# State space stage: gating by VectorE through PSUM, the second step-width chain and each group's end spread over later rounds, scaling by ScalarE

## The reference

```python
proj = x @ W_in.T                        # 256 -> 8512 = 4096 (z) + 4352 (xBC) + 64 (dt)
z, xBC, dt = split(proj)
xBC = silu(causal_depthwise_conv(xBC, taps=4) + conv_b)
xs, B, C = split(xBC)                    # 4096 = 64 heads x 64, 128, 128
dt = softplus(dt + dt_bias);  A = -exp(A_log)
# per head: y_t = sum_{s<=t} (C_t . B_s) exp(sum_{s<r<=t} dt_r A) dt_s x_s
y = y + D * xs
g = y * silu(z)
out = (g * rsqrt(mean(g*g, -1) + 1e-5) * norm_w) @ W_out.T     # 4096 -> 256
x = layernorm(x + out)
```

## Time and profile before

| | |
|---|---|
| three timed runs | 4166.07, 4168.1 (median), 4176.48 us |
| the profiled execution | 4173.8 us, of which span 4172.0 us |
| the stage's acc matmuls, first and last start | 2845.5 and 3803.7 us |
| PE / DVE / ACT / POOL busy over the span | 87% / 71% / 46% / 36% |
| mean granted TensorE clock | 0.928 of 2.4 GHz |

### The profile page before, as it was taken

One profiled execution on the slowest core, in us unless ns is written; L12 is line 12 of the kernel. 1 busy time (PEld: TensorE's weight loads), 2 busy tenths in 40 slices (PEclk: granted clock), 3 DMA queues, 4 the chain that ended last, 5 costly groups with the idle time before them and its releaser, 6 DMA issues.

```text
span 4172.0 us, 65936 instructions
## 1 busy us (share of the span) xinstructions
PE 3614.6 (87%) x23748; PEld 2230.1 (53%) x23762; DVE 2960.1 (71%) x6387; ACT 1925.4 (46%) x4723; POOL 1481.8 (36%) x1336
## 2 busy tenths in 40 slices
PE   7799999998981868789999979879989999997885
PEld 3466666665651436644555555555555555554544
DVE  7799989988659674533555658857777777775678
ACT  4466666665532324312333324435545555553345
POOL 2533213333302000000111123017979888895220
PEclk9899999999985989989999989899999999997887
DMA  2222222222200100020000000302211112121000
GB/s 70 64 70 67 55 65 66 65 64 50 50 14 30 34 23 2 2 75 22 1 1 1 1 31 2 126 8 79 76 61 72 71 66 71 66 72 68 1 1 21
DMA packets 240578, 185.94 MB, mean 45 GB/s; under 512 B 117632, under 2 KB 216576, under 8 KB 239168
## 3 DMA queue, kind: packets, MB, share of 16 engines
q1 hardware_dynamic: 240256, 181.73, 14.4%
HBM read 166.45 MB, written 15.20 MB: 44 GB/s over the span
## 4 chain that ended last, share of the span: by engine, by line
PE 43%; DVE 22%; issue 16%; POOL 13%; ACT 4%; SPq 1%; DMA 1%; POOLq 0%; DVEq 0%; ACTq 0%
PE ps L310 10%; POOL mE L3365 7%; POOL mSQ L3376 4%; PE ps L2161 3%; PE ps L2886 3%; PE ps L2899 3%; PE ps L2865 2%; PE ps L502 2%; PE ps L2196 1%; PE ps L2679 1%; PE ps L580 1%; PE ps L1972 1%; DVE hMX L2954 1%; PE ps L316 1%; ACT lP L2260 1%
## 5 line engine op out<-in xcount | busy, mean ns | idle before, releaser
L310 PE MATMUL ps<-xT,min 128*128 128x512 f32 (+1 forms) x1072 | 499.1, 612 | 8.4 <-DVE macc L3307 7.7
L3307 DVE SCALAR_TENSOR_TENSOR macc<-ps,mcw,macc 128x508 f32<-128x508 f32 (+2 forms) x408 | 302.9, 742 | 183.6 <-ACT macc L3242 173.9
L3369 POOL TENSOR_TENSOR macc<-macc,mZ 128x512 f32<-128x512 f32 x128 | 384.8, 3006 | 70.3 <-DVE macc L3320 65.5
L3365 POOL TENSOR_TENSOR mE<-mE,mCB 128x1024 f32<-128x1024 f32 x128 | 307.9, 2407 | 18.0 <-ACT mCB L3253 15.8
L310 PEld LDWEIGHTS ps<-xT,min 128*128 128x128 f32 (+1 forms) x1072 | 191.8, 191 | 227.1 <-issue 210.8
L3181 PE MATMUL ps<-mwo,macc 128*128 128x256 f32 x1024 | 261.7, 400 | 42.4 <-POOL macc L3369 37.6
L3317 DVE TENSOR_TENSOR_SCAN mE<-mE,mid 128x1024 f32<-128x1024 f32 x128 | 295.1, 2306 | 0.0
L2351 POOL TENSOR_TENSOR lP<-lP,lm 128x512 f32<-128x512 f32 x64 | 66.6, 1041 | 574.5 <-DVE lm L2324 574.5
L826 POOL TENSOR_TENSOR dTB<-did,dNB 128x1024 f32<-128x1024 f32 (+1 forms) x10 | 29.3, 2928 | 661.7 <-DMA dNB<-d_N 597.6
L2924 ACT ACTIVATE hE<-ps 128x512 f32<-128x512 f32 x256 | 139.0, 594 | 222.2 <-PE ps L2886 222.2
L3181 PEld LDWEIGHTS ps<-mwo,macc 128*128 128x128 f32 x1024 | 188.3, 194 | 93.9 <-POOL macc L3369 72.2
(11 more groups left out here) (573 smaller groups left out, 8605.7 us busy)
## 6 DMA issues: line engine op xcount, KB each, us to landing
mE<-m_decay SPq DMA_DIRECT2D x128, 512.0 KB, 3.6
dwk<-in_L_attn_Wk SPq DMA_DIRECT2D x64, 128.0 KB, 2.3
dwq<-in_L_attn_Wq SPq DMA_DIRECT2D x64, 128.0 KB, 2.3
dwv<-in_L_attn_Wv SPq DMA_DIRECT2D x64, 128.0 KB, 2.4
dwg<-in_L_attn_Wg SPq DMA_DIRECT2D x64, 128.0 KB, 2.4
dwo<-in_L_attn_Wo SPq DMA_DIRECT2D x64, 128.0 KB, 2.6
min<-in_m_in SPq DMA_DIRECT2D x2, 4096.0 KB, 18.2
d_N<-dNT SPq DMA_DIRECT2D x256, 16.0 KB, 1.5
```

The source lines that it names most:

```text
L310: t = pe.matmul(out, w[:, j, :], self.c.xT[:, j, blk(g, 512)], start=j == 0, stop=j == 1)
L3307: x = dve.scalar_tensor_tensor(out=acc[:, :, 3 - j:T], in0=p[:, :, 0:T - 3 + j], scalar=self.cw[:, i, j:j + 1], in1=acc[:, :, 3 - j:T], op ...
L3365: pool.tensor_tensor(E, E, bc(self.CB[g % 2][:, :, :].rearrange("p b t -> p (b t)"), 2), ALU.mult).then_inc(*self.em.up)
L3369: pool.tensor_tensor(self.acc[s][:, :], self.acc[s][:, :], self.Z[s][:, :], ALU.mult).then_inc(*self.ys.up)
```

## The change

1. **Gate.** VectorE now writes yd (L3338) into bank 7 in place and then multiplies bank 7 by Z into acc (L3342). GpSimd's gate goes. Bank 7 is free for the next y only after the gate.
2. **Order of a round.** sq stands on ScalarE between z and x, no longer at the end. The group's small steps stand before "tr" and "taps", not behind "y".
3. **End of a group.** The eleven instructions become a step "rsq" of their own; close, rsq, sums, stats, rsqrt, scale stand 4, 5, 7, 9, 11 and 12 rounds after the group's last entry. Scaling is four ScalarE instructions with scale and bias; one DVE instruction computes the bias (-mean times rsqrt).
4. **Chain 1.** Its pieces stand in rounds 3 to 20 (table LATE), one per round; the reciprocal is four pieces of 128 columns. The turn of the last group of x and both dt projections use banks 4 and 5, and the turn moves to round 2. Its DMA store is issued before unit 24, not unit 3.
5. **Start.** Chain 0 runs alone and waits for nothing of chain 1. -exp(A_log) is made by ScalarE. GpSimd scales W_out before it waits for the stage ahead.

```diff
+    LATE = {2: ("turn", 1), 3: ("dt", 1), 4: ("exp", 1), 6: ("chain", 0), 7: ("ln", 1), 8: ("chain", 1), ...
+            11: ("chain", 4), ... 16: ("chain", 9), 18: ("decays", 1),
+            20: ("parts", 1)}
...
-            if u in (-1, 3):
+            if u in (-1, 24):
...
-            for step, q in (("yd", t - 3), ("x2", t - 1), ("em", t - 1), ("z", t), ("x", t), ("close", t - 4), ("cb", t - 1), ("decay", t),
-                            ("tr", t - 1), ("taps", t), ("sq", t - 3), ("acc", t - 3), ("y", t - 2), ("sums", t - 4), ("stats", t - 5),
-                            ("rsqrt", t - 6), ("scale", t - 7)):
+            for step, q in (("yd", t - 3), ("x2", t - 1), ("em", t - 1), ("z", t), ("sq", t - 3), ("x", t), ("close", t - 4), ("cb", t - 1),
+                            ("decay", t), ("rsq", t - 5), ("sums", t - 7), ("stats", t - 9), ("rsqrt", t - 11), ("scale", t - 12),
+                            ("tr", t - 1), ("taps", t), ("acc", t - 3), ("y", t - 2)):
...
-                room[7] = self.yd.at(u + 1)
+                room[7] = self.ys.at(u + 1)
...
+            elif step == "scale":
+                act.wait_ge(*self.off.at(g + 1))
+                for j in range(4):
+                    x = act.activation(c.X[:, 4 * g + j, :], c.R[:, j, :], ACT.Identity, scale=c.rsq[:, j:j + 1], bias=c.rsq[:, 12 + j:13 + j])
+                x.then_inc(*c.xn.up)
...
+            elif k < 7:
+                then(dve.reciprocal(d[:, blk(k - 3)], d[:, blk(k - 3)]))
...
-                dve.scalar_tensor_tensor(out=self.acc[s][:, :], in0=self.acc[s][:, :], scalar=self.s[:, 34 + i:35 + i], in1=bank(7),
+                dve.scalar_tensor_tensor(out=bank(7), in0=self.acc[s][:, :], scalar=self.s[:, 34 + i:35 + i], in1=bank(7),
                                          op0=ALU.mult, op1=ALU.add).then_inc(*self.yd.up)
+                dve.wait_ge(*self.zt.at(u + 1))
+                dve.wait_ge(*self.yd.at(u + 1))
+                dve.tensor_tensor(self.acc[s][:, :], bank(7), self.Z[s][:, :], ALU.mult).then_inc(*self.ys.up)
...
+            elif step == "rsq":
+                dve.wait_ge(*self.smv.at(g + 1))
+                last = c.rsqrt_rest(dve, own, [self.sw[:, blk(n, 4)] for n in range(3)])
             elif step == "sums":
...
+                if g:
+                    dve.wait_ge(*c.xn.at(4 * self.n + g))
...
     def gpsimd(self, pool, own):
         c = self.c
-        pool.wait_ge(*c.xn.at(4 * self.n))
         pool.wait_ge(self.dma[0], 80)
         pool.wait_ge(self.dma[2], 16)
...
+        self.before(pool)
...
-            elif step == "yd":
-                pool.wait_ge(*self.yd.at(u + 1))
-                pool.wait_ge(*self.zt.at(u + 1))
-                pool.tensor_tensor(self.acc[s][:, :], self.acc[s][:, :], self.Z[s][:, :], ALU.mult).then_inc(*self.ys.up)
```

More of the change, by code:

```diff
@@ L3026 @@
     PLACE, REST, EARLY, LOADS = 71296, 0, True, 10
+    LATE = {2: ("turn", 1), 3: ("dt", 1), 4: ("exp", 1), 6: ("chain", 0), 7: ("ln", 1), 8: ("chain", 1), 9: ("chain", 2), 10: ("chain", 3),
+            11: ("chain", 4), 12: ("chain", 5), 13: ("chain", 6), 14: ("chain", 7), 15: ("chain", 8), 16: ("chain", 9), 18: ("decays", 1),
+            20: ("parts", 1)}
     def weights(self):
@@ L3105, in order @@
                         yield step, q, units[q], g, i
-                elif step in ("close", "sums", "stats", "rsqrt", "scale"):
+                elif step in ("close", "rsq", "sums", "stats", "rsqrt", "scale"):
                     if i == 31:
@@ L3110, in order @@
                     yield step, q, units[q], g, i
-                if (step, t) in (("x", 0), ("taps", 2)):
-                    yield "parts", t // 2, 0, 0, 0
+                if step == "x" and t == 0:
+                    yield "parts", 0, 0, 0, 0
+                if step == "taps" and t in self.LATE:
+                    yield *self.LATE[t], 0, 0, 0
     def gone(self, q):
@@ L3120, in tensor, with dt @@
         pe.wait_ge(self.dma[0], 80)
[L3121 to L3124, removed]
+        def dt(n):
+            pe.wait_ge(*room[4])
             pe.wait_ge(*c.xt_ready(self.n, 2 * n + 1))
             for e in range(2):
-                t = self.columns(pe, bank(n)[blk(e, 64), :], self.w[:, :, 8448:8512], 2 * n + e)
+                t = self.columns(pe, bank(4)[blk(e, 64), :], self.w[:, :, 8448:8512], 2 * n + e)
             t.then_inc(*self.dm.up)
-            room[n] = self.rel.at(n + 1)
+            room[4] = self.rel.at(n + 1)
+        dt(0)
         pe.wait_ge(self.dma[1], 32)
@@ L3132, in tensor @@
             s, to = q % 4, 4 * (g % 2)
-            if step == "parts":
+            if step == "turn":
+                c.turn_tensor(pe, self.n - 1, 3, (4, 5))
+            elif step == "dt":
+                dt(1)
+            elif step == "parts":
                 x = self.chain[q][0]
@@ L3226, in scalar @@
                 act.copy(to, bank(4).rearrange("p (j e h) -> p j e h", j=4, e=2)).then_inc(*self.cols.up)
-            elif step == "chain":
-                if q == 1:
-                    decay(1)
+            elif step == "turn":
+                c.turn_scalar(act, self.n - 1, 3, (4, 5))
+            elif step in ("dt", "exp", "ln", "decays"):
+                chain(step, 1)
+            elif step == "scale":
[3 more added lines that the diff above has]
+                x.then_inc(*c.xn.up)
             elif step == "z":
@@ L3293, in chain @@
                 dve.tensor_tensor(x, x, d, ALU.add).then_inc(*self.dtx.up)
-        dve.wait_ge(*self.aexp.at(1))
-        then(dve.tensor_scalar(self.ah[:, 1:2], self.ah[:, 0:1], -1.0, None, ALU.mult))
-        for k in range(2):
+        for k in range(10):
             chain(0, k)
@@ L3339, in vector @@
                 dve.wait_ge(own.sem, last)
-                last = c.rsqrt_of(dve, own, c.st, c.rsq, 1e-5)
-            elif step == "scale":
-                dve.wait_ge(own.sem, last)
-                c.scale_vector(dve, g, c.R)
+                dve.wait_ge(own.sem, c.rsqrt_of(dve, own, c.st, c.rsq, 1e-5))
+                dve.scalar_tensor_tensor(out=c.rsq[:, 12:16], in0=c.st[:, :, 6:7].rearrange("p a b -> p (a b)"), scalar=-1.0, in1=c.rsq[:, 0:4],
+                                         op0=ALU.mult, op1=ALU.mult).then_inc(*self.off.up)
     def gpsimd(self, pool, own):
         c = self.c
-        pool.wait_ge(*c.xn.at(4 * self.n))
         pool.wait_ge(self.dma[0], 80)
```

65 lines of the change are left out of this document (32 added, 33 removed).

## The result

The changed kernel takes 4115.4 us (median of 4 runs, 4111.85 to 4118.62) against 4167.1 beside it (4161.99 to 4176.48): ratio 0.9872, 95% interval 0.9859 to 0.9885, so 51.7 us less where 48.5 were forecast (4120). Its profiled execution took 4114.33 us, span 4112.5, mean granted clock 0.930.

The account below looks back on a forecast made before the run. A nearly full PE waiting on POOL's gate, in the ring gate, acc, y, yd, was taken as the bound. Gains 24.7 + 11.5 + 5.5 + 1.8 + 9 - 4 = 48.5 us off median 4168.1 gave 4120, range 4090 to 4152.

Parts of the forecast that it names:

- What bounds before: In regular rounds nearly full PE waits for POOL's gate, which lies still during DVE's scan; waits 69.7 us in all.
- Regular rounds: 97 regular distances between neighbouring acc loads shrink by 0.255 us each, to 6.88: gain 24.7 us.
- DVE fits: In a regular round DVE needs 6.1 of 6.88 us, with gate 0.70 and yd 0.75; PE stays the limit.
- Ends of groups: Three group ends go from 141.9 to 130.4 us, PE stalling 8 a group: gain 11.5 (bounds 7 and 26.5).
- B and C: Rounds over B and C at the three group ends, where PE lacks work: gain 5.5 us over three.
- last three: Last three rounds, the bare ring of acc, y, yd and gate: 0.6 us less each, 1.8 in all.
- chain 1: Its pieces on DVE in rounds 4 to 16, six having to wait behind em: cost 4 us (0 to 8).
- Start: Before the first acc: chain 0 ends 9.8 us earlier, chain 1 gives 1.3, turn costs 2; gain 9 (5 to 12).
- Scaling: ScalarE's four scalings fall in idle time, but cost +0.7 us at the stage's very end; last gate gives 0.6 back.
- Nearly no contention: Rival, 27%: DVE and POOL hardly contend; group ends gain 26.5 us, chain 1 costs nothing, time 4100.
- DVE as the bound: Rival, 13%: gate and yd cost 0.3 to 0.5 us more together, a DVE round reaching 7.0; time 4143.
- The scan behind em: Slower rival, 7%: DVE's scan waits for POOL's em every round, deciding from 1.03 us; round 7.55, time 4199.

## Why the prediction was right

- *What bounds before.* Right: taking only the gate off POOL removes the wait from the regular rounds and makes every one of them 6.82.
- *Regular rounds.* Mechanism right, size low: 0.31 a round, not 0.255, 30.4 us in place of 24.7, and 6.82 lies outside the 6.85 to 6.9 that it named as its sign. The prediction took off 0.015 for a weight load that it thought exposed, and read the early case from a close round, where acc loads 0.38 us after the first tr matmul; in a regular round it is 2995.43 - 2995.10 = 0.33. From 0.65 that is 0.32.
- *DVE fits.* Right: 0.69 and 0.75 as taken, DVE idle 0.69 us a round ahead of the taps.
- *Ends of groups.* The step mis-sized: 4.9 us in place of 11.5, outside the bounds of 7 to 26.5. What PE loses per group (12.2, 11.2, 11.2, less 1.26 for close) comes to 10.3 on average, not 8, and more than the 9.5 given for full contention. "Contention nearly each time" was really each time, and for two instructions of each chain: rsq takes 5.2 and rsqrt 5.6 us of DVE's time, near the upper ends given (5.7 and 6). Of the loss behind rsq in the first group (6.3 us over two rounds) only 3.3 is waiting; the rest goes with the lower clock behind it. Moving the steps takes 23.7 of these 30.8 us away, so the cause is shown.
- *Which steps contend.* The prediction says that the small steps and chain pieces have two SBUF inputs. The four that waited at the group ends (L205 and L207 in rsq, L196 and L205 in rsqrt) have one. The first chain had no contention in the kernel before (0.16 and 0.17); the change itself brought it, by the gate's move as well as by the new place.
- *B and C* 6.8 for 5.5, *last three* 1.6 for 1.8, *chain 1* 3.3 for 4: near what was worked out. The change of order has a part in B and C that the prediction did not name: 2.7 of the 6.8 go without it.
- *Start.* 9.8 for 9. Chain 0 alone ends 9.6 earlier, 9.8 as it was worked out; the rest is small.
- *Scaling.* ScalarE's four take 2.07 us at the very end of the stage, where VectorE took 1.38: +0.7 as taken. No run tests this last term alone.
- *Rivals.* Nearly no contention: wrong here; the version with the small steps ahead of the scan comes near it. DVE as the bound: no. The scan behind em: absent after the change, present with the gate alone, at 0.97 us just short of deciding.

The two errors, +5.7 and -6.6, nearly cancel; that the time came within 5 us of the 4120 forecast is in part luck.

## What to carry to other kernels

When two engines share an interface, look where in a round the other one is idle and put small, dependent instructions there; in this kernel spreading them helped little until they stood there. A chain of dependent instructions can lose its turn to the other engine where one waits for another. An order is tuned for the engine that does a step: with the gate left on GpSimd the rest of this change made the kernel 1.3% slower, so the parts of this change could not be judged one by one.

## What the runs showed of the hardware

- The waiting time stands inside the record of the waiting instruction: 128x4 at 1.17 or 2.27 us in place of 0.16, with no idle time before it, so no table of waits lists it. It was found by comparing the same line's time between places.
- Between two chained VectorE instructions GpSimd goes ahead with 2.35 us of work, although only 0.03 us lie between their records (2995.20 + 1.18 = 2996.38, the next at 2996.41): em started at 2996.31, when the squares were done.
- In rsq's stall 3.3 us of waiting cost TensorE 6.3: the granted clock was 0.50 to 0.53 for about 6 us behind it, from 3072 to 3078.
- VectorE's statistics (L222, one SBUF input) are not held up: 1.38 us beside POOL's squares, 1.40 with POOL idle.

```profile
3097.00 1.72 POOL L3395 TENSOR_TENSOR mSQ<-mSQ,mtn 128x512 f32<-128x512 f32 x1 [2.19 <-ACT mtn L3283]
3097.57 1.38 DVE L222 BATCH_NORM_STATS2 st<-R 128x6 f32<-128x256 f32 x4
...
3751.58 1.40 DVE L222 BATCH_NORM_STATS2 st<-R 128x6 f32<-128x256 f32 x4
```
